# A message-passing edge stage: fp32r scatter products one step later, edge attributes split before the transpose, window sums of two groups in one PSUM bank

## The reference, cut to what matters

```python
src, dst = (edge_index[0], edge_index[1])
ei = jnp.concatenate([x[src], edge_attr], axis=-1)          # 256 + 64
core = jnp.maximum(ei @ W1 + b1, 0.0) @ W2 + b2
gate = jax.nn.sigmoid(ei @ Wg + bg)
msg = gate * core
agg = jax.ops.segment_sum(msg, dst, num_segments=x.shape[0])
out = agg + x                                                # then layer norms
```

## Time and profile before

| | |
|---|---|
| median of 3 runs | 2724.02 us (2723.71 to 2724.32) |
| the profiled execution | 2720.98 us, of which the span from first to last instruction is 2719.2 us |
| PE busy | 2456.6 us, 90% of the span |
| DVE busy | 2122.3 us, 78% |
| POOL busy | 1392.3 us, 51% |
| ACT busy | 1198.6 us, 44% |
| TensorE clock granted, mean | 0.964 of full |

### The profile page before, as it was taken

How to read it: one execution, slowest core, us unless ns; L and a number is a source line. 1 busy time by engine, 2 the same in 40 slices (tenths; PEclk the granted TensorE clock), 3 DMA queues, 4 the chain that set the end, 5 groups by cost and what they waited for, 6 DMA issues and landing times. The chain is left out here.

```text
span 2719.2 us, 50207 instructions
## 1 busy us (share of the span) xinstructions
PE 2456.6 (90%) x15657; PEld 1890.4 (70%) x15657; DVE 2122.3 (78%) x5332; ACT 1198.6 (44%) x2210; POOL 1392.3 (51%) x1385
## 2 busy tenths in 40 slices
PE   6879999999999999999999994789999967888874
PEld 3469999999999999999999983245555533444453
DVE  6658888888889899899999998997988852333357
ACT  1145555555555555555555552453766730000035
POOL 0046555555555555555555441465666727777720
PEclk9989999999999999999999997999999988999987
DMA  6555555555555555555555553254465667555442
GB/s 211 206 148 152 161 156 157 157 157 157 155 157 157 157 171 166 157 171 168 171 164 170 166 163 97 77 134 125 130 163 153 164 195 252 194 180 198 152 139 95
DMA packets 302010, 435.20 MB, mean 160 GB/s; under 512 B 152850, under 2 KB 223908, under 8 KB 299220
## 3 DMA queue, kind: packets, MB, share of 16 engines
q0 software_dynamic: 90368, 281.11, 35.6%
q1 hardware_dynamic: 202120, 136.24, 17.0%
q10 hardware_dynamic: 9292, 14.90, 1.6%
HBM read 361.34 MB, written 70.80 MB: 159 GB/s over the span
## 5 line engine op out<-in xcount | busy, mean ns | idle before, releaser
L687 POOL DMA_INDIRECT gathered<-p_table,src_t x784 | 777.9, 992 | 812.6 <-DVE gate L1552 500.7
L687 POOL DMA_INDIRECT gathered<-hop_table,src_t x576 | 581.4, 1009 | 387.6 <-issue 148.3
L1134 ACT ACTIVATE hidden_hi<-banks 128x512 fp32r<-128x512 f32 x392 | 234.6, 599 | 565.6 <-PE banks L830 565.6
L853 PE MATMUL banks<-w_hi,hidden_hi 128*128 128x256 f32 x1568 | 459.8, 293 | 0.0
L853 PE MATMUL banks<-w_lo,hidden_hi 128*128 128x256 f32 x1568 | 443.5, 283 | 0.0
L853 PE MATMUL banks<-w_hi,hidden_lo 128*128 128x256 f32 x1568 | 443.3, 283 | 0.0
L866 PE MATMUL banks<-room,hot 128*128 128x257 f32 x1568 | 373.9, 380 | 6.4 <-DVE room L1561 6.1
L1221 ACT CAST counts<-banks 128x686 f32 (+3 forms) x382 | 295.7, 774 | 180.6 <-PE banks L922 80.3
L1541 DVE SCALAR_TENSOR_TENSOR hidden_lo<-banks,hidden_hi 128x512 fp32r<-128x512 f32 x392 | 266.1, 689 | 117.9 <-ACT hidden_hi L1134 117.1
L922 PE MATMUL banks<-codes,low_hot 128*128 128x343 f16 (+3 forms) x958 | 241.0, 332 | 79.3 <-DVE codes L1777 63.0
L866 PEld LDWEIGHTS banks<-room,hot 128*128 128x128 f32 x1568 | 282.8, 189 | 41.7 <-DVE room L1561 8.9
(11 more groups left out here) (209 smaller groups left out, 4452.9 us busy)
## 6 DMA issues: line engine op xcount, KB each, us to landing
counts_saved<-counts SPq DMA_DIRECT2D x20, 1568.0 KB, 9.4
ring<-counts_saved SPq DMA_DIRECT2D x20, 1568.0 KB, 7.4
ea<-in_edge_attr SPq DMA_DIRECT2D x196, 128.0 KB
gathered<-p_table,src_t POOLq DMA_INDIRECT x784
p_table<-p_t ACTq DMA_DIRECT2D x48, 256.0 KB, 3.7
hop_table<-parts SPq DMA_DIRECT2D x12, 896.0 KB
gathered<-hop_table,src_t POOLq DMA_INDIRECT x576, 2.8
x_saved<-x_room SPq DMA_DIRECT2D x7, 896.0 KB, 5.4
```

Source lines behind the costliest of these rows:

```text
L687: pool.indirect_dma_start(out=rows[:, n % slots, j, :], out_offset=None, in_=table[:, :], in_offset=bass.IndirectOffsetOnAxis(ap=src_t[:, ...
L853: last = nc.tensor.matmul(banks[:, 4 + half, j % 2 * H:(j % 2 + 1) * H], lhs, rhs, start=False, stop=n == len(products) - 1, skip_group_ch ...
L1134: nc.scalar.activation(hidden_hi[:, k, :], banks[:, k, :], ACT.Relu).then_inc(S["hidden_upper"], 1)
```

## The change

- PE: `scatter` makes, for each tile, two fp32r products: one-hot (`hot_window`, now fp32r) by the message's upper half with its ones (258 columns), and by its lower half (256 columns). It runs one step later (lag -1), for 197 steps.
- ACT: new `upper_msg`, a cast of each half of the message into `msg_hi`, one before each `upper_hidden`; the latter is cut in two stages.
- The lower half `msg_lo`: half 0 of each group by POOL, between the gathers; half 1 by DVE, a step later, after `add_window`.
- Edge attributes are split before the transpose: ACT `round_ea` (128 x 256 from SBUF), DVE `lower_ea` (one instruction, 128 x 256), both four groups ahead; PE turns [upper, lower] of each tile, four transposes; ACT `copy_ea` copies the bank (128 x 512).
- `add_window` runs another step later. For groups 78 to 159 (`paired`) two groups are summed in bank 6 before it runs; the base block of such a pair is the lower one. The check of spans takes pairs together for the first 160 groups.
- Node work of a chunk begins two groups later (`begins`).
- The loop for the ones becomes one copy; in setup, DVE has two more small instructions.

```diff
+        begins = [g + 2 for g in complete]
+        paired = range(begins[0], 2 * PAIRED)
+        def in_pair(g):
+            return isinstance(g, int) and g in paired
+        def adds_until(g):
+            if isinstance(g, int) and g > paired.start:
+                return g - (min(g, paired.stop) - paired.start + 1) // 2
+            return g
...
-                wait_count(sp, S["ea_turned"], g - 1)
+                wait_count(sp, S["ea_split"], g - 1)
...
+            def lower_msg(g):
+                pool.wait_ge(S["msg_upper"], 2 * g + 1)
+                nc.gpsimd.tensor_tensor(msg_of(msg_lo, g % 2, 0), msg_of(msg, g % 2, 0), msg_of(msg_hi, g % 2, 0).bitcast(F32),
+                                        ALU.subtract).then_inc(S["msg_split0"], 1)
             for g in range(NG):
+                if g >= 3:
+                    lower_msg(g - 3)
                 gather(p_table, gathered, 2, 0, "p_gathered", "gate_added", 2, g)
                 if g % PLACES == PLACES - 1 and g // PLACES < NC:
                     add_beta(g // PLACES)
+            for g in range(NG - 3, NG):
+                lower_msg(g)
...
             def turn_ea(turn, s, g):
-                pe.wait_ge(S[f"ea_loaded{s}"], 16 * (turn + 1))
-                wait_count(pe, S["ea_ready"], 2 * g)
-                for q in range(2):
-                    last = nc.tensor.transpose(banks[:, 7, q * P:(q + 1) * P],
-                                               ea[:, s, 2 * q:2 * q + 2, :].rearrange("p j d -> p (j d)"), ident[:, :])
+                pe.wait_ge(S["ea_split"], g + 1)
+                wait_count(pe, S["ea_ready"], g)
+                for j in range(TILES):
+                    last = nc.tensor.transpose(banks[:, 7, j * P:(j + 1) * P],
+                                               ea_split[:, s, j, :, :].bitcast(F32).rearrange("p b d -> p (b d)"), ident[:, :])
                 last.then_inc(S["ea_turned"], 1)
...
+            def scatter(turn, s, g):
+                pe.wait_ge(S["hot_ready"], g + 1)
+                opens, closes = not (in_pair(g) and s), not (in_pair(g) and not s)
+                if opens:
+                    wait_count(pe, S["agg_added"], adds_until(g))
+                for j in range(TILES):
+                    u = TILES * s + j
+                    if j % 2 == 0:
+                        pe.wait_ge(S[f"msg_split{j // 2}"], g + 1)
+                    nc.tensor.matmul(banks[:, 6, 0:HP], hot_window[:, u, :], msg_hi[:, u, :], start=opens and j == 0, stop=False,
+                                     skip_group_check=True)
+                    nc.tensor.matmul(banks[:, 6, 0:H], hot_window[:, u, :], msg_lo[:, u, :], start=False,
+                                     stop=closes and j == TILES - 1, skip_group_check=True).then_inc(S["scattered"], 1)
...
-                    at_tiles(lambda *tile: scatter_stage(msg_of, HD, msg_is_ready, "", *tile), i, s, 0)
+                    at_group(scatter_stage, i, s, -1)
                     at_group(turn_ea, i, s, 3)
...
+            def round_ea(turn, s, g):
+                act.wait_ge(S[f"ea_loaded{s}"], 16 * (turn + 1))
+                wait_count(act, S["ea_turned"], g - 1)
+                nc.scalar.copy(ea_split[:, s, :, 0, :], ea[:, s, :, :]).then_inc(S["ea_rounded"], 1)
+            def copy_ea(turn, s, g):
                 act.wait_ge(S["ea_turned"], g + 1)
                 wait_count(act, S["gate_product"], 2 * (g - 1))
-                for odd in range(2):
-                    nc.scalar.copy(ea_pieces(s, odd, True), ea_bank(odd)).then_inc(S["ea_rounded"], 1)
+                nc.scalar.copy(ea_turned_sb[:, s, :], banks[:, 7, :]).then_inc(S["ea_ready"], 1)
...
+            def upper_msg(half):
+                def stage(turn, s, g):
+                    act.wait_ge(S["msg_ready"], 2 * g + half + 1)
+                    nc.scalar.copy(msg_of(msg_hi, s, half), msg_of(msg, s, half)).then_inc(S["msg_upper"], 1)
...
             def step(i, s):
-                at_group(upper_ea, i, s, 2)
-                at_group(upper_hidden, i, s, 1)
+                at_group(copy_ea, i, s, 2)
+                at_group(round_ea, i, s, 4)
+                at_group(upper_msg(0), i, s, 0)
+                at_group(upper_hidden(0), i, s, 1)
+                at_group(upper_msg(1), i, s, 0)
+                at_group(upper_hidden(1), i, s, 1)
                 at_group(seed_core, i, s, 1)
                 at_group(open_gate, i, s, 1)
...
+            then(nc.vector.tensor_tensor(base_f[0:PAIRED, 0:1], base_f[0:PAIRED, 0:1], base_f[0:PAIRED, 1:2], ALU.min))
+            then(nc.vector.tensor_tensor(top_f[0:PAIRED, 0:1], top_f[0:PAIRED, 0:1], top_f[0:PAIRED, 1:2], ALU.max))
...
             def lower_ea(turn, s, g):
-                for odd in range(2):
-                    dve.wait_ge(S["ea_rounded"], 2 * g + odd + 1)
-                    nc.vector.tensor_tensor(ea_pieces(s, odd, False), ea_bank(odd),
-                                            ea_pieces(s, odd, True).bitcast(F32), ALU.subtract).then_inc(
-                        S["ea_ready"], 1)
+                dve.wait_ge(S["ea_rounded"], g + 1)
+                nc.vector.tensor_tensor(ea_split[:, s, :, 1, :], ea[:, s, :, :], ea_split[:, s, :, 0, :].bitcast(F32),
+                                        ALU.subtract).then_inc(S["ea_split"], 1)
...
+            def lower_msg(turn, s, g):
+                dve.wait_ge(S["msg_upper"], 2 * g + 2)
+                nc.vector.tensor_tensor(msg_of(msg_lo, s, 1), msg_of(msg, s, 1), msg_of(msg_hi, s, 1).bitcast(F32),
+                                        ALU.subtract).then_inc(S["msg_split1"], 1)
...
+            def add_window(turn, s, g):
+                if in_pair(g):
+                    if s == 0:
+                        return
+                    s, g, end = 0, g - 1, g + 1
+                else:
+                    end = g + 1
...
-                at_tiles(lambda *tile: add_window(HD, "", *tile), i, s, -1)
+                at_group(add_window, i, s, -2)
+                at_group(lower_msg, i, s, -1)
                 node_work_at(0)
-                at_tiles(lambda *tile: one_hot("", *tile), i, s, 0)
+                at_group(lower_ea, i, s, 4)
                 node_work_at(1)
-                at_group(lower_ea, i, s, 2)
+                at_group(message, i, s, 0)
+                at_group(one_hot, i, s, 0)
                 node_work_at(2)
-                at_group(message, i, s, 0)
                 at_group(lower_hidden(0), i, s, 1)
                 at_group(lower_hidden(1), i, s, 1)
```

205 lines of the change are left out of this document (78 added, 127 removed).

## The result

The changed kernel takes 2717.15 us, median of 11 runs (2707.56 to 2725.02), against 2723.71 us of the kernel before in the same hours (11 runs, 2722.06 to 2727.38): a ratio of 0.9973, 95% interval 0.9962 to 0.9984. It is 6.6 us faster by the medians, 0.16 to 0.38% by the interval. The forecast was 2673 us, so 44 us of the forecast gain did not come.

The account below looks back on a forecast made before the run. TensorE sets the edge stage's pace, VectorE close behind. Group gains, less 15 us for beta and 4.5 for the ends, come to 51.0 us: 2720.98 to 2670, or 2673 as median; range 2608 to 2725.

Parts of the forecast that it names:

- PE: TensorE per group: scatter gains 0.77 us, edge transposes add 0.22, so 7.58 becomes 7.03 us.
- GpSimd's operation: Half message remainder put between GpSimd's gathers: 1.17 us a group, 6.6 us in all, inside 7.0.
- Rival C: GpSimd becomes the bound if its new operation is dear: at 2.6 us, 116 us slower, 2840; chance 0.13.
- Beta: Seven beta adds on GpSimd, groups 7 to 55, no longer have room: 2.1 to 2.2 us lost each, 15 us.
- The loop through ScalarE: VectorE and ScalarE hand over remainders and casts in turn: a loop of 6.95 us, just under PE's 7.03.
- Pairs: VectorE, groups 78 to 159: one window add per two groups, in two goes, saves 0.45 us a group.
- 6.5 + 0.83 N: Loop time per group in pairs, with node work: 6.9, 7.1, 7.3 us; without pairs 6.95 + 0.83 N.
- N: VectorE's node work per group, busy less 6.24: 0.47 to 1.21 us, five of six pieces in the loop.
- The lock: VectorE instructions with two SBUF inputs and GpSimd ones reading SBUF exclude each other; counted at 0.07 us per group.
- The ends: Pipeline one step longer, 4 us at the end, plus 0.5 in set-up; the start hides: 4.5 us lost.
- Rival B: Loop through ScalarE dearer, or lock strikes each group: 7.4 not 7.1 us, 2713 at worst, 2700 middle; chance 0.17.

Follow-up runs that it names:

- e2: Changed kernel with beta added in 49 pieces of 256 elements, groups 7 to 55, instead of seven of 1792; 2697.62 us, ratio 0.9923.
- e5: Changed kernel with VectorE making both halves of the message remainder and GpSimd none; 2703.42 us, ratio 0.993.
- e14: Changed kernel without pairs, a window add for every group; 2713.39 us, ratio 0.9967.
- e16: Changed kernel with beta in tiles, node pieces moved behind the gate add, hidden before message on ScalarE, and no pairs; 2654.64 us, ratio 0.9748.
- e3: Changed kernel with GpSimd subtracting only 4 of 256 columns per tile, the scatter using the other half's remainder; 2668.78 us, ratio 0.9813.
- e6: Changed kernel with GpSimd writing 128 x 512 twice instead of subtracting, that half of the remainders left out; 2679.37 us, ratio 0.9843.
- e15: Changed kernel with beta in tiles, node pieces behind the gate add, hidden before message and edge rounding before copying on ScalarE; 2646.11 us, ratio 0.9722.

## Why the prediction was wrong in size

**PE, right.** 7.03 us a group was forecast; undisturbed groups take 7.00 to 7.02. Scatter products come 0.12 apart and the four transposes take 0.35, as said.

**GpSimd's operation, right.** 1.17 us forecast, 1.20 measured (median 1204 ns of 196). It was put at 5.3 to 6.5 after the end of the gate add; in the steady group above that end is 598.56 and the operation runs 603.82 to 605.02. Rival C, in which GpSimd becomes the bound, did not come.

**Beta, right in size.** 15 us forecast, 15.8 by e2. The mechanism was another in part: it was costed as late gathers, and the rows show 18.6 us of VectorE's message remainders standing behind beta adds. The sum of the first 78 groups came out 5.7 us better than forecast.

**The loop through ScalarE, put too long.** The wait at the second hidden remainder was forecast at 0.5 us, and the rows show 0.32, with 0.24 at the first. But the loop was put at 6.95 us, and e5 adds 0.60 us to it and still has groups of 7.0: without the addition it is at most some 6.5 us. The sum took ScalarE's four steps at 0.60 each, and in the trace they start 0.50 apart (602.05, 602.54, 603.05, 603.54 in the steady group). This error made the forecast too cautious, and so hid a part of the miss.

**Pairs, wrong.** 0.45 us a group in groups 108 to 159 stood in the loop's 6.5 + 0.83 N. e14 prices it at nothing, and e16 at 7 us where the lock hardly strikes. The working took the saved time of one engine as time of the loop, without asking what VectorE waits for next: ScalarE's rounding, 0.41 us of work behind a copy of 0.57.

**The lock, the step that failed.** The forecast had the row that shows it, the one-hot of 0.99 us, and had the time at which GpSimd's operation comes. It then put the operation "beside operations that read PSUM", which it took from the steady state, and counted 0.07 a group. That holds for a group without node work. But five of the six places of node work stand in the loop, as the forecast itself had counted for N, and two of them stand beside that very moment; the pieces there have their operands in SBUF. At 0.07 for 87 groups that is 6 us; the standstill measured there is 38. The forecast's periods for groups 108 to 194 add up to 651.8 us, the measured ones to 694.0, a miss of 42.2, with e3's at 659.3 and e6's at 663.0: the lock, with the waits and the falls of the clock that come with it, carries 31 to 35 of the 42. The other 7 to 11 were not split among pairs, node work and the rest.

**The ends.** 4.5 us forecast. Measured are 7.0 at the stage's ends and 3.9 behind it. 4.2 of the 7.0 lie at the start, which the forecast had put at nothing. Where the 3.9 went was not followed.

Rival B named both mechanisms, and its "lock strikes each group" would have given 2713 at worst. What came was neither of its clauses: the lock did not strike each group but those with node work, and there for up to 1.7 us. The arithmetic of the whole: 55.5 us forecast for the groups, 17.7 measured, so 37.8 of the missing 44; the ends and what lies behind make 6.4. That the first 78 groups came out 5.7 us better covers a part of the late groups' miss.

The version that comes out, e15, computes everything at 2646.1 us: 2.8% under the kernel before, and 71 us under the changed one. It has the same operations on the same engines. Beta is cut in tiles, pieces stand where GpSimd's operation does not run, and ScalarE takes the next group's hidden layer before this group's messages.

## What to carry to other kernels

When work is moved to GpSimd, its duration is the smaller half of the price. Lay its interval over VectorE's timeline in every stage of the kernel, not only in the steady one, and look at what each VectorE instruction there reads and writes; a 0.15 us instruction here took up to 1.7 us. Where the GpSimd operation stands right behind a gather in its queue, begin its interval some 0.6 us before the recorded start.

In a loop that runs through two engines, time saved on one is gain only up to the next wait. Try removing a cost and moving it before adding up savings, and test two small edits together: the order on ScalarE brought 5 to 6.5 us while the pieces stood in their old places, and 31 us once they had moved.

## What the runs showed of the hardware

**Which VectorE instructions stand still.** Counted in the changed kernel from 160 to 1640 us, of instructions that overlap a GpSimd tensor operation by over 0.1 us: those with two tensor inputs, both in SBUF, 47 of 59 were lengthened, by 52.2 us (18.6 of it around the beta adds); tensor-scalar instructions with one input and the output in SBUF, 18 of 19, by 12.3 us; those with an input in PSUM, none of 424, though their other input and their output lie in SBUF; batch-norm instructions, none of 27. One of the latter beside GpSimd's operation (VectorE, then GpSimd):

```profile
1297.35 0.42 DVE L1659 BATCH_NORM_STATS2 stats<-agg 128x6 f32<-128x256 f32 x1
```
```profile
1296.59 1.19 POOL L698 TENSOR_TENSOR msg_lo<-room,msg_hi 128x512 fp32r<-128x512 f32 x1
```

**Who wins.** Where GpSimd had been idle and VectorE's one-hot had begun 0.22 us before, four times, the one-hot kept its 0.68 us and GpSimd's operation took 1.50 instead of 1.20. VectorE, then GpSimd:

```profile
1205.44 0.68 DVE L1584 TENSOR_TENSOR hot_window<-iota,lo_t 128x512 fp32r<-128x512 f32 x1
```
```profile
1205.66 1.50 POOL L698 TENSOR_TENSOR msg_lo<-room,msg_hi 128x512 fp32r<-128x512 f32 x1 [0.22 <-ACT msg_hi L1141]
```

Where GpSimd's operation stands right behind a gather in its queue, an earlier recorded start does not help. Of the instructions of the two lengthened kinds, 16 began 0.03 to 0.59 us before it, and 15 of them were held to its end; of 22 that began 0.62 to 0.97 us before, none was. This one, alone over in about 0.16 us, would have ended before GpSimd's began:

```profile
1001.78 1.64 DVE L1647 SCALAR_TENSOR_TENSOR term<-term,squares 128x14 f32<-128x14 f32 x1
```
```profile
1002.18 1.20 POOL L698 TENSOR_TENSOR msg_lo<-room,msg_hi 128x512 fp32r<-128x512 f32 x1
```

So the stretch in which VectorE can be held is then about 1.8 us, not 1.2. Why is not shown.

**Writes lock less.** In e6, beside GpSimd's write-only instructions, none of 53 instructions with two SBUF inputs was lengthened (seven others stood behind beta adds), but 9 of 15 tensor-scalar ones were, by 0.2 us each. The Trainium skill (SBUF — State Buffer, Who interferes with whom) says that an instruction with two SBUF inputs contends only with a GpSimd instruction that reads SBUF, that one in a two-port mode contends with GpSimd, and that whichever issues first blocks the other for the whole instruction. The counts agree with the first point. They agree with the second if the tensor-scalar instructions ran in such a mode, which no row tells. By the recorded starts the third holds where GpSimd had been idle, and not right behind a gather, unless GpSimd's operation issues some 0.6 us before its recorded start.

**Gathers are held too.** Of the changed kernel's gathers from 160 to 1640 us, 162 began inside a VectorE instruction with two SBUF inputs that had over 0.25 us left; all took over 1.05 us, 1.19 in the median. 195 began inside one that reads PSUM, and none did; the usual time is 0.95. In the kernel before it is 119 of 119 against none of 186, and the 1.18 us of the gather at 601.16 in the earlier trace rows is one of them: a one-hot ran from 600.83. In the steady group of the changed kernel (GpSimd, then VectorE):

```profile
600.10 1.19 POOL L679 DMA_INDIRECT gathered<-p_table,src_t  x1 [0.30 <-issue]
```
```profile
600.04 0.43 DVE L1545 TENSOR_TENSOR ea_split<-ea,ea_split 128x256 fp32r<-128x256 f32 x1
```
